# Joining two layer-norm stages and the sign projection between them into one stage

## What is computed

```python
x = x + ga * _L0_attn_ref(h, ...)
h = _layernorm(x, axis=-1) * (1 + cb) + sb
x = x + gb * _L0_ffn_ref(h, L0_ffn_weight, L0_ffn_scale_param)
# second layer
h = _layernorm(x, axis=-1) * (1 + ca) + sa
q = (h @ Wq.T + bq); k = (h @ Wk.T + bk); v = (h @ Wv.T + bv)
# _L0_ffn_ref:
out = jnp.einsum('bsi,oi->bso', input, binary_weight)
out = out * row_scale[None, None, :] * scale_param[None, None, :]
return jnp.nan_to_num(out, nan=0.0, posinf=1000000.0, neginf=-1000000.0)
```

## Time and profile before

| | us |
|---|---|
| median of three runs | 2402.07 |
| lowest, highest | 2399.64, 2402.64 |
| the profiled execution | 2398.61 |
| its span, first to last instruction | 2396.9 |
| TensorE busy in the span | 2025.7 (85%) |
| VectorE busy | 1501.5 (63%) |
| GpSimd busy | 1085.8 (45%) |
| ScalarE busy | 1039.6 (43%) |

### The profile page before, as it was taken

How to read it: one execution, slowest core, us unless ns; L and a number is a source line. 1 busy time by engine, 2 the same in 40 slices (tenths; PEclk the granted TensorE clock), 3 DMA queues, 4 the chain that set the end, 5 groups by cost and what they waited for, 6 DMA issues and landing times. The chain is left out here.

```text
span 2396.9 us, 34177 instructions
## 1 busy us (share of the span) xinstructions
PE 2025.7 (85%) x11760; PEld 1648.7 (69%) x11760; DVE 1501.5 (63%) x3703; ACT 1039.6 (43%) x2408; POOL 1085.8 (45%) x846
## 2 busy tenths in 40 slices
PE   7389999999999994297836999999999999636786
PEld 1278888888888873175425888888888888525654
DVE  1566666666666667925655666666666666785274
ACT  1255555555555551224124555545555555303322
POOL 0455545555455543543126545545545455346121
PEclk9699999999999996698967999999999999867898
DMA  6300001000010000226230001000010010013441
GB/s 242 115 18 27 18 27 45 19 27 19 27 45 19 27 18 31 97 87 120 50 120 27 18 27 45 19 27 19 27 45 19 27 42 21 23 43 103 105 94 49
DMA packets 129765, 118.57 MB, mean 49 GB/s; under 512 B 43172, under 2 KB 95396, under 8 KB 128564
## 3 DMA queue, kind: packets, MB, share of 16 engines
q1 hardware_dynamic: 111764, 93.92, 13.6%
q10 hardware_dynamic: 17824, 22.40, 2.9%
HBM read 95.29 MB, written 16.81 MB: 47 GB/s over the span
## 5 line engine op out<-in xcount | busy, mean ns | idle before, releaser
L996 POOL TENSOR_TENSOR gqa_rot<-gqa_rot,consts 128x512 f32<-128x512 f32 x160 | 209.4, 1309 | 640.4 <-ACT gqa_rot L817 640.2
L833 ACT ACTIVATE gqa_prob<-gqa_prob,gqa_nmax 128x128 f32<-128x128 f32 (+3 forms) x512 | 281.9, 552 | 198.5 <-DVE gqa_nmax L918 198.5
L918 DVE CUSTOM_DVE_ANT_0 gqa_prob<-gqa_pS,consts 128x128 f32<-128x128 f32 (+3 forms) x512 | 220.2, 486 | 73.8 <-PE gqa_pS L717 72.9
L926 DVE TENSOR_TENSOR gqa_ptl<-gqa_pT,gqa_pth 128x384 fp32r<-128x384 f32 (+1 forms) x384 | 218.2, 596 | 32.0 <-ACT gqa_pth L843 27.2
L843 ACT CAST gqa_pth<-gqa_pT 128x384 fp32r<-128x384 f32 (+1 forms) x384 | 182.5, 510 | 94.6 <-PE gqa_pT L732 94.5
L999 POOL TENSOR_TENSOR gqa_full<-gqa_full,gqa_rot 128x512 f32<-128x512 f32 x160 | 206.5, 1291 | 12.6
L771 PE MATMUL gqa_pW<-woh,gqa_oh 128*128 128x512 f32 x504 | 202.7, 402 | 9.0 <-DVE y L943 9.0
L459 PE MATMUL ln_pT<-consts,ln_xn 128*128 128x128 f32 x192 | 45.4, 423 | 190.2 <-DVE ln_xn L438 190.2
L690 PE MATMUL gqa_pj<-first_hh,wqh 128*128 128x512 f32 x496 | 205.7, 415 | 0.0
L1008 POOL TENSOR_TENSOR gqa_ql<-gqa_full,gqa_qh 128x512 fp32r<-128x512 f32 x128 | 164.3, 1284 | 73.0 <-DVE gqa_qh L907 73.0
L771 PE MATMUL gqa_pW<-woh,gqa_ol 128*128 128x512 f32 x504 | 197.3, 392 | 0.0
(11 more groups left out here) (206 smaller groups left out, 5122.8 us busy)
## 6 DMA issues: line engine op xcount, KB each, us to landing
raw_q<-in_wq SPq DMA_DIRECT2D x16, 1024.0 KB, 5.3
raw_o<-in_wo SPq DMA_DIRECT2D x16, 1024.0 KB, 5.2
mod_wm<-in_wmod SPq DMA_DIRECT2D x8, 1536.0 KB, 19.3
raw_kv<-in_wkv SPq DMA_DIRECT2D x16, 512.0 KB, 6.6
x<-in_x SPq DMA_DIRECT2D x4, 1024.0 KB, 6.5
kp<-qkv_rest SPq DMA_DIRECT2D x16, 256.0 KB, 2.3
qp<-qkv_rest SPq DMA_DIRECT2D x16, 256.0 KB, 2.3
vp<-qkv_rest SPq DMA_DIRECT2D x64, 64.0 KB, 1.8
```

What stands on the lines that cost most here:

```text
L833: ins = nc.scalar.activation(p, p, ACT.Exp, scale=-1.0, bias=nmax[r][:, i:i + 1], accum_out=den[r][:, i:i + 1])
L918: nc.vector.tensor_tensor_reduce(prob[r][:, P_OFF[i]:P_OFF[i] + w], pS[s][:, c:c + w], held.mask[:, T - w:T], -1.0, LARGEST, ALU.add, ALU.min,
L926: nc.vector.tensor_tensor(ptl[:, c:c + w], pT[k % 2][:, 0:w], pth[:, c:c + w].bitcast(F32), ALU.subtract).then_inc(pt_lo, 1)
L996: nc.gpsimd.tensor_tensor(rot[r % 2][:], rot[r % 2][:], held.sinT, ALU.mult).then_inc(sined, 1)
```

## The change

`stage_middle` takes the place of `stage_norm` (residual=0), `stage_sign_ffn` and `stage_norm` (residual=1). Two tiles of four PSUM banks each are in use at once: pT for transposes, pF for products. A pass i = 0 to 3 of the norm belongs to batch i % 2, and to the first norm for i < 2, to the second for i >= 2.

- VectorE does both batches' first residual and statistics, then per batch examines four tiles and adds their second residual, then the second statistics. It folds the mean into a shift (one more small operation), makes half of the variance first (another), and has a Newton step of three operations instead of four: 12 linked steps instead of 15 for four tiles.
- The normalised tile is written by ScalarE, into y; ScalarE reads each transposed PSUM block twice, once for hf and once for hh. All low parts are on GpSimd.
- What is no number is marked by a not_equal on VectorE and replaced by a second copy_predicated from a tile of zeros, which a memset fills at the stage's start; GpSimd's product is gone.
- The second gate is applied by GpSimd for all eight tiles.
- All loads are issued by SyncE at the stage's start; the sign weights are loaded into hf's buffer. The gates of the second residual are loaded in the same stage, once the first are used.

```diff
-def stage_sign_ffn(nc, held, a, signs, half):
+def stage_middle(nc, held, a, hf, signs, qkv, later, half):
...
             @block.sync
             def _(sp):
+                signs.load(sp)
+                qkv.load(sp)
+                for loaded in later:
+                    loaded.load(sp)
+                sp.wait_ge(own_gated, HB)
+                sp.wait_ge(gated, NT - HB)
                 load_gates(sp, held, a, 1, half, gate_in)
+                for loaded in later:
+                    loaded.landed(sp)
+
+            @block.gpsimd
+            def _(pool):
+                def low(i, ks):
+                    b = batch(i)
+                    t = slice(b * T, (b + 1) * T)
+                    for k in ks:
+                        pool.wait_ge(h_hi, i * KT + k + 1)
+                        nc.gpsimd.tensor_tensor(hl[:, k, t], hf[:, k], hh[:, k, t].bitcast(F32), ALU.subtract).then_inc(h_lo, 1)
+
+                def apply_gate(j):
+                    pool.wait_ge(put, j + 1)
+                    pool.wait_ge(gate_in, 16 * HB)
+                    nc.gpsimd.tensor_tensor(y[:, j, :], y[:, j, :], gate[:, j // TT, :], ALU.mult).then_inc(z_gated, 1)
+
+                for j in range(NT):
+                    if j % TT:
+                        nc.gpsimd.tensor_tensor(y[:, j, :], y[:, j, :], gate[:, j // TT, :], ALU.mult).then_inc(gated, 1)
+                low(0, range(KT))
+                low(1, range(KT))
+                for j in range(TT):
+                    apply_gate(j)
+                qkv.los(pool)
+                for j in range(TT, NT):
+                    apply_gate(j)
+                low(2, range(KT))
+                low(3, range(KT))
+
+            @block.vector
+            def _(dve):
...
+                def second_residual(j):
+                    dve.wait_ge(z_gated, j + 1)
+                    summed(1, j)
+
+                def normalise(i, b):
...
+                    link(nc.vector.tensor_scalar(v, mv[:, i, s, 1], EPS, None, ALU.add))
+                    nc.vector.tensor_scalar(h, v, -0.5, None, ALU.mult)
+                    link(nc.vector.tensor_scalar(t.bitcast(I32), v.bitcast(I32), 1, None, ALU.logical_shift_right))
+                    link(nc.vector.tensor_scalar(r.bitcast(I32), t.bitcast(I32), -1.0, float(MAGIC), ALU.mult, ALU.add))
+                    for _ in range(NEWTON):
+                        link(nc.vector.tensor_tensor(t, r, r, ALU.mult))
+                        link(nc.vector.tensor_tensor(t, t, h, ALU.mult))
+                        link(nc.vector.scalar_tensor_tensor(r, t, 1.5, r, ALU.add, ALU.mult))
+                    nc.vector.scalar_tensor_tensor(m, mv[:, i, s, 0], -1.0, r, ALU.mult, ALU.mult).then_inc(ready, 1)
+
+                def examine(j):
+                    dve.wait_ge(full, j + 1)
+                    nc.vector.tensor_tensor(y[:, j], pF[j % 4][:], rs[:], ALU.mult).then_inc(z_done, 1)
+                    dve.wait_ge(z_done, j + 1)
+
+                    nc.vector.tensor_tensor(nan[j % 2][:], y[:, j], y[:, j], ALU.not_equal).then_inc(marked, 1)
+                    nc.vector.tensor_scalar(clip[j % 2][:], y[:, j], LIMIT, -LIMIT, ALU.min, ALU.max).then_inc(marked, 1)
+                    nc.vector.tensor_scalar(wild[j % 2][:], y[:, j], 0.0, 0.0, ALU.mult, ALU.not_equal).then_inc(marked, 1)
+                    dve.wait_ge(marked, 3 * j + 3)
+                    nc.vector.copy_predicated(y[:, j], wild[j % 2][:], clip[j % 2][:]).then_inc(replaced, 1)
+                    dve.wait_ge(replaced, j + 1)
+                    nc.vector.copy_predicated(y[:, j], nan[j % 2][:], zeros[:]).then_inc(put, 1)
+
+                nc.vector.memset(zeros[:], 0.0).then_inc(cleared, 1)
+                dve.wait_ge(cleared, 1)
+                for b in range(HB):
+                    for j in range(b * TT, (b + 1) * TT):
+                        first_residual(j)
+                    normalise(0, b)
+                for b in range(HB):
+                    for j in range(b * TT, (b + 1) * TT):
+                        if j % TT >= 2:
+                            dve.wait_ge(put, j - 1)
+                        examine(j)
+                        if j % TT >= 2:
+                            second_residual(j - 2)
+                    second_residual(b * TT + 2)
+                    second_residual(b * TT + 3)
+                    normalise(1, b)
 
             @block.tensor
             def _(pe):
...
+                turn(0)
+                signed(0)
+                signed(1)
+                turn(1)
+                for j in range(2, NT):
+                    signed(j)
+                turn(2)
+                turn(3)
+
+            @block.scalar
+            def _(act):
+                def features(i):
+                    b, layer, ci = batch(i), i // HB, 2 * (1 - i // HB)
+                    act.wait_ge(ready, i + 1)
+                    for j in range(b * TT, (b + 1) * TT):
+                        nc.scalar.activation(y[:, j, :], x[:, j, :], ACT.Identity, bias=shift[:, i // HB, j:j + 1],
+                                             scale=rstd[:, i // HB, j:j + 1]).then_inc(xn_done, 1)
+                    act.wait_ge(turned, i + 1)
...
+                    for k in range(KT):
...
+                        nc.scalar.activation(hf[:, k], pT[k][:], ACT.Identity, **by).then_inc(scaled, 1)
+                        nc.scalar.activation(hh[:, k, t], pT[k][:], ACT.Identity, **by).then_inc(h_hi, 1)
+
+                signs.his(act)
+                features(0)
+                features(1)
+                qkv.his(act)
+                features(2)
+                features(3)
```

More of the change, by code:

```diff
@@ L1045, in _, with turn @@
             @block.tensor
             def _(pe):
-                for j in range(NT):
+                def turn(i):
+                    b = batch(i)
+                    if i:
+                        pe.wait_ge(h_hi, i * KT)
+                    for j in range(TT):
+                        pe.wait_ge(xn_done, i * TT + j + 1)
+                        for k in range(KT):
+                            mm = pe.transpose(pT[k][:, j * P:(j + 1) * P], y[:, b * TT + j, k * P:(k + 1) * P], held.ident)
+                    mm.then_inc(turned, 1)
@@ L1048, in _, with signed @@
+                def signed(j):
+                    pe.wait_ge(signs.signed, KT)
+                    pe.wait_ge(h_lo, (j // TT + 1) * KT)
+                    if j >= 4:
+                        pe.wait_ge(z_done, j - 3)
                     for k in range(KT):
-                        for n, hp in enumerate((held.hh, held.hl)):
-                            mm = pe.matmul(ps[j][:], hp[:, k, j * P:(j + 1) * P], sgn[:, k, :],
+                        for n, hp in enumerate((hh, hl)):
+                            mm = pe.matmul(pF[j % 4][:], hp[:, k, j * P:(j + 1) * P], sgn[:, k, :],
@@ new lines, in _ @@
+            @block.scalar
[7 more added lines that the diff above has]
+                    act.wait_ge(turned, i + 1)
+                    t = slice(b * T, (b + 1) * T)
+                    if i >= HB:
+                        act.wait_ge(full, (b + 1) * TT)
+                    for k in range(KT):
+                        by = {"bias": held.modh[:, layer, ci, k, b:b + 1], "scale": held.modh[:, layer, ci + 1, k, b:b + 1]}
+                        if i:
+                            act.wait_ge(h_lo, (i - 1) * KT + k + 1)
+                        nc.scalar.activation(hf[:, k], pT[k][:], ACT.Identity, **by).then_inc(scaled, 1)
[6 more added lines that the diff above has]
+                features(3)
@@ L1653, in build @@
                         stage_groups(nc, held, a, wts, g * GB)
[L1654 to L1657, removed]
             with ExitStack() as octx:
@@ L1664, in build @@
                     qkv = QkvWeights(qctx, nc, a)
-                    stage_norm(nc, held, a, 1, 0, half, residual=1, ahead=qkv, later=(gates, out, lora))
+                    with ExitStack() as sctx:
+                        hf = sctx.enter_context(nc.sbuf_tensor("mid_hf", [P, KT, T], F32))
+                        signs = SignWeights(sctx, nc, a, hf)
+                        stage_middle(nc, held, a, hf, signs, qkv, (gates, out, lora), half)
                     stage_qkv(nc, held, a, qkv, kd0, gates)
```

60 lines of the change are left out of this document (49 added, 11 removed).

## The result

The changed kernel takes 2372.62 us in the median of four runs (2370.03 to 2375.59), the kernel before 2402.18 in the median of its four. The ratio is 0.9879, with a 95% interval from 0.9862 to 0.9897: 1.2% faster. The forecast was 2375 (2366 to 2390). In a second set, timed with e1, e2 and e9, it took 2373.3 against 2399.41 us, ratio 0.9893 (0.9876 to 0.9909).

The account below looks back on a forecast made before the run. Between head groups and QKV it saw a VectorE chain with holes and serial tails; joined stages of 97.0 us against 111.5 and 110.1 save 27 us: 2371.6 profiled, 2375 as median, range 2366 to 2390.

Parts of the forecast that it names:

- First pass: Joined stage's start: batch 0's normalisation ready at 12.7 us, VectorE free after batch 1's at 25.6 us.
- Down to the first product: Batch 0 through ScalarE, transposes and low parts to the sign product: first product full at 27.7 us.
- Examine: VectorE's check of each sign-product tile: 3.5 us alone, more for tiles 1 and 2 beside GpSimd's queue.
- Holds: VectorE waiting on GpSimd for SBUF: about 1 us per short or 512-wide port operation meeting queued GpSimd work.
- Batch 1 and the tail: Stage's end: tiles and residuals 21.0 us, to 79.8; normalisation 5.2, to 85.0; uncovered tail 12.0, to 97.
- The sum: Joined stage 97.0 us against 111.5 and 110.1: 14.5 + 13.1 = 27.6 us saved, taken as 27.
- boundaries only: Rival: in-order queues lose the overlap, only empty starts gain, 11.6 us, 2390.5; chance 0.15 together with gates on the path.
- The second rival: Every GpSimd operation holds VectorE its whole length, +13 us per half: 2400.5 us, no change; chance 0.07.
- the loads: Weight loads at the stage's start, issued by SyncE instead of ScalarE: move costed at nothing.

Follow-up runs that it names:

- e1: The changed kernel without its second predicated copy, so what is no number is not replaced by zero: 2362.91 us, stages 90.8 and 91.0 us.
- e2: The changed kernel with GpSimd's four low parts of pass 2 waiting for VectorE's last normalisation: 2372.37 us, stages 94.3 and 94.3 us.
- e9: The kernel before, with GpSimd's product replaced by a second predicated copy on VectorE in its separate sign stage: 2398.81 us.
- e5: The changed kernel with four stages of one tiny memset put ahead of each joined stage: 2378.33 us, 1.0 us a boundary.
- e7: The changed kernel with the eight second-gate multiplies on VectorE instead of GpSimd: 2382.68 us, stages 101.2 and 101.1 us.
- e8: The changed kernel with GpSimd's product in place of the second predicated copy: 2383.92 us, stages 102.1 and 101.7 us.
- e10: The changed kernel with e2's edit, the last stage's loads issued by ScalarE, and the last pass's features shared with VectorE: 2364.8 us, ratio 0.9853.

## Why the prediction was right, point by point

The prediction's clock starts at VectorE's first operation, 907.82 in the profile.

- *First pass.* Ready of batch 0 at 12.7: measured 12.3. VectorE free at 25.6: 25.0. The removed boundaries were put at 0.8 us each; e5 shows 1.0.
- *Down to the first product.* Full at 27.7, after a hole of 2.1 us: 27.3 and 2.3. Batch 1's transposes were put at an end of 32.4 and ended at 30.9, since TensorE's clock rose during the first tile and not during the second.
- *Examine.* Tile 0 3.5 us: 3.6. Tiles 1 and 2 were put at 4.5 and 8.2 us: 6.5 and 6.1, because the low parts came 1.5 us sooner. The sum is 12.6 against 12.7; that the errors of the two tiles cancel was luck. The end of tile 2 was put at 44.0: 43.5. The second copy at 0.61 + 0.13: 0.74 us in the median.
- *Holds.* I charged about 16 us per half. Adding up in the profile what VectorE's operations on SBUF alone take above 0.69, 0.42, 0.74 and 0.17 us after the first pass of batch 0 gives 15.7 us, in 20 operations. e2 shows the price directly; e7 shows that a GpSimd operation taken away need not take its hold away.
- *Batch 1 and the tail.* 79.8 to the end of the residuals: 79.0; normalisation 5.2: 4.9. The tail at 12.0: 12.3 (991.76 to 1004.07).
- *The sum.* 97.0 us per stage against 96.3 and 96.6; 27 us in all against 28.8 in the profile and 29.6 between the medians. I had rounded 27.6 down to 27 without need. I kept the time outside as it was, and in the profile it was 4.6 us longer, so the profiled execution was put at 2371.6 and took 2374.36; this difference is inside the scatter of the kernel's four runs.

The rival "boundaries only" had the gate chain of GpSimd 7 us late. Gate 0 was done at about 948 and wanted at 951.27: the reserve was 3 us, and e1 and e8 show what happens where it is gone. The second rival expected each GpSimd operation to hold VectorE for its whole length. The trace shows that VectorE pays at most about the rest of the GpSimd operation that runs when it asks (0.34 to 1.11 us in the 20 holds), and nothing while it is in bn_stats (0.69 us) or reads PSUM (0.68 us): 15.7 us and not 29.5. The Trainium skill (SBUF — State Buffer, Who interferes with whom) says no more than that: whichever of the two issues first has the shared pair for its whole instruction, and a VectorE instruction with at most one SBUF input, outside the 2-port perf modes, does not contend. The trace agrees with both; my reading of the page as a price per GpSimd operation was stricter than its words.

What I sized wrong: the loads. I wrote that their move costs nothing, and did not write that leaving them would have cost 8 us; and the gain of e9 was put at 1.4 us per stage and was 0.6, as I had not counted the last two tiles' extra copies at the end.

## What to carry to other kernels

Before joining stages, write the schedule of the binding engine in order and add, for each of its operations that a helper engine's operations hold, the rest of the one helper operation that runs when it asks: here this gave a 97 us stage to within 1 us. A helper engine with an in-order queue is cheap only for work that nobody wants soon; the same replacement was worth 1 us in separate stages and 11 us in the joined one, because there it stood behind four low parts. Move the issue of loads away from the head of an engine's queue as soon as that engine enters the path, and look for the tail in which the binding engine has nothing to do: work held back until then (e2) or shared with it (e10) is nearly free.

## What the runs showed of the hardware that was not expected

TensorE's granted clock fell after a short pause. The windows, in the changed kernel's first half, are around the first products, the products of tiles 2 and 3, those of tile 4 and part of 5 after a pause of 4.15 us, and those behind them (columns as in the first fence):

```profile
932.00:934.30 2.30, 2.30 (x6) 1.76 (x6) 0.72 (x5) 1.41 (x2) 0.00 (x0) 0.50 0.00 0
938.80:942.20 3.40, 3.40 (x16) 2.60 (x14) 3.33 (x5) 3.40 (x6) 1.93 (x2) 1.00 0.00 0
946.60:951.40 4.80, 4.80 (x12) 3.74 (x13) 4.73 (x6) 3.81 (x8) 2.93 (x2) 0.50 0.00 0
952.00:956.40 4.40, 4.40 (x20) 3.37 (x18) 4.30 (x8) 0.00 (x0) 1.16 (x2) 1.00 0.00 2
```

After 11 us in which it worked almost without a break, the last eight at 2.4 GHz, TensorE paused from 942.4 to 946.5, until batch 1's last low part was done, and came back at 1.2 GHz for five microseconds. It cost nothing, since VectorE reads tile 4's product only at 965.65. Also, in e10 VectorE's read of PSUM with two per-partition operands took 0.80 and 0.81 us for 512 columns, where its multiply of PSUM with an SBUF tile takes 0.68.
